# A graph and attention layer on one core: more buffers and later register reads in the routed stage, and both count matrices zeroed by SyncE

## What is computed

```python
xn = layernorm(x)
# two graph convolutions with symmetric normalisation and self loops
gnn = D^-1/2 (A+I) D^-1/2 relu(D^-1/2 (A+I) D^-1/2 xn W1 + b1) W2 + b2
# linear attention, 12 heads, 256 random features, then projection and layernorm
x = x + gnn + layernorm(xn + attention(xn) W_proj + b_proj) * gamma + beta
h = layernorm(x)
e = max(index of the two largest of h @ router_w)      # one of 8 experts per row
x = x + silu(h @ w1[e]) @ w2[e]
```

## Time and profile before

| | |
|---|---|
| median of 3 runs | 2644.51 us (2637.38 to 2648.0) |
| the profiled execution's own time | 2640.27 us |
| its span, first to last instruction | 2638.3 us |
| PE busy | 2413.7 us, 91% of the span |
| DVE, ACT, POOL busy | 1386.8, 802.2, 835.6 us |
| mean granted PE clock | 0.962 of full speed |
| DMA | 474.16 MB, mean 180 GB/s |

### The profile page before, as it was taken

One profiled execution on the slowest core, in us unless ns is written; L12 is line 12 of the kernel. 1 busy time (PEld: TensorE's weight loads), 2 busy tenths in 40 slices (PEclk: granted clock), 3 DMA queues, 4 the chain that ended last, 5 costly groups with the idle time before them and its releaser, 6 DMA issues.

```text
span 2638.3 us, 44428 instructions
## 1 busy us (share of the span) xinstructions
PE 2413.7 (91%) x16483; PEld 1628.1 (62%) x16483; DVE 1386.8 (53%) x2865; ACT 802.2 (30%) x1093; POOL 835.6 (32%) x587
## 2 busy tenths in 40 slices
PE   4889899999999999998899999999998899999376
PEld 2676768686866666666565566666664566666354
DVE  6575848583666767666313444444540444444343
ACT  3333324342364744646011222222220011111132
POOL 2133343435888888871000000000000000000265
PEclk9989989999999999999999999999998999999699
DMA  9976969654423233230432999999975844444186
GB/s 387 404 256 181 356 218 336 190 157 115 110 14 61 2 60 38 22 60 1 157 75 99 289 296 300 286 285 300 280 232 217 272 166 166 170 165 148 43 161 116
DMA packets 184192, 474.16 MB, mean 180 GB/s; under 512 B 74864, under 2 KB 81882, under 8 KB 174460
## 3 DMA queue, kind: packets, MB, share of 16 engines
q1 hardware_dynamic: 93596, 340.86, 36.6%
q0 software_dynamic: 79664, 101.99, 21.0%
q10 hardware_dynamic: 10800, 29.50, 2.9%
HBM read 266.99 MB, written 210.77 MB: 181 GB/s over the span
## 4 chain that ended last, share of the span: by engine, by line
PE 62%; DVE 13%; DMA 12%; ACT 6%; issue 4%; SPq 1%; POOL 0%; DVEq 0%; ACTq 0%; POOLq 0%
PE pair L1792 30%; PE pair L368 24%; DVE arena L1162 4%; DMA arena<-in_w_qkv 2%; PE pair L1617 2%; PE pair L1565 2%; DVE arena L1267 2%; DVE arena L1269 2%; DVE arena L1273 2%; DMA arena<-hl_dram,arena 2%; ACT arena L871 2%; DMA arena<-in_g_t 2%; PE pair L1628 1%; DMA arena<-in_ffn_in 1%; DMA arena<-ahl_dram 1%
## 5 line engine op out<-in xcount | busy, mean ns | idle before, releaser
L368 PE MATMUL pair<-arena 128*128 128x384 f16 (+2 forms) x5760 | 914.0, 320 | 27.6 <-SPq L357 7.2
L1792 PE MATMUL pair<-arena 128*128 128x384 f16 x4900 | 820.5, 328 | 25.9 <-DMA arena<-ahl_dram 11.8
L368 PEld LDWEIGHTS pair<-arena 128*128 128x128 f16 (+1 forms) x5760 | 570.0, 99 | 357.5 <-issue 34.0
L700 POOL DMA_INDIRECT cells<-arena x392 | 649.0, 1656 | 383.4 <-DMA cells<-arena 228.3
L1792 PEld LDWEIGHTS pair<-arena 128*128 128x128 f16 x4900 | 475.9, 98 | 336.3 <-issue 15.4
L1617 PE MATMUL pair<-arena 128*128 128x256 f32 x600 | 173.8, 425 | 18.9 <-ACT arena L810 18.9
L734 POOL DMA_INDIRECT slots<-arena x25 | 28.8, 1152 | 492.6 <-DVEq L1491 460.0
L1628 PEld LDWEIGHTS pair<-arena 128*128 128x128 f32 x1200 | 155.7, 197 | 20.1 <-ACT arena L835 15.1
L1628 PE MATMUL pair<-arena 128*128 128x66 f32 x1200 | 155.5, 278 | 11.1 <-ACT arena L835 11.0
L1162 DVE SCALAR_TENSOR_TENSOR arena<-arena 128x256 f16<-128x256 f32 x392 | 161.5, 479 | 4.7 <-DVE arena L1086 4.4
L722 POOL DMA_DIRECT2D arena<-cells x25 | 30.3, 1213 | 421.5 <-DMA arena<-cells 421.5
(11 more groups left out here) (195 smaller groups left out, 2270.4 us busy)
## 6 DMA issues: line engine op xcount, KB each, us to landing
cells<-arena POOLq DMA_DIRECT2D x25, 1600.0 KB, 11.1
cells<-arena SPq DMA_DIRECT2D x25, 1600.0 KB, 12.3
arena<-cells SPq DMA_DIRECT2D x25, 1600.0 KB, 9.6
arena<-cells POOLq DMA_DIRECT2D x25, 1600.0 KB, 13.2
ahl_dram<-arena SPq DMA_DIRECT2D x25, 1600.0 KB, 13.4
arena<-ahl_dram SPq DMA_DIRECT2D x25, 1600.0 KB, 7.6
arena<-in_x SPq DMA_DIRECT2D x70, 384.0 KB, 5.3
arena<-key_dram SPq DMA_DIRECT2D x28, 896.0 KB, 5.6
```

Of the source, the lines that this page charges most:

```text
L368: ins = nc.tensor.matmul(dst[half], left(k, a), right(k, b, half), start=start and n == 0, stop=stop and n == 2)
L700: nc.gpsimd.indirect_dma_start(cells[k], bass.IndirectOffsetOnAxis(ap=idx_all[:, m:m + 1], axis=0), val_all[:, m:m + 1], None, bounds_chec ...
L1792: ins = nc.tensor.matmul(pair[u][:, half, 0:HD], a[:, 0, s * P:(s + 1) * P], X[part][:, s, half * HD:(half + 1) * HD], start=(s == 0 and p ...
```

## The change

Three edits in one:

1. The routed stage has six gather buffers (NG) and four result buffers (NO). POOL issues gather(0..5) first, then for each j: add(j), gather(j+6). The buffers are zeroed as float32 (768 elements) and not as float16 (1536).
2. PE reads three expert registers before the first turn and each later one between an up and a down.
3. POOL zeroes nothing. SP issues all 50 strips in the 18 pairs of chunks 0 to 2, two or three after each weight load, matrix 0 first. Scatters start when matrix 0 is zero; BOTH is 4. Semaphores are shared in another way.

```diff
-BOTH = 8
+BOTH = 4
+CLEAR_CHUNKS = 3
+NG, NO = 6, 4
...
+            sp.wait_ge(consts, 2)
             for c in range(C):
...
-                    if c in (1, 2):
-                        for n in range(T * m // (2 * PAIRS) - T // 2, T * (m + 1) // (2 * PAIRS) - T // 2):
-                            clear_tile(sp, 1, n).then_inc(cleared_other, 16)
+                    if c < CLEAR_CHUNKS:
+                        for i in range(2 * T * m // (CLEAR_CHUNKS * PAIRS), 2 * T * (m + 1) // (CLEAR_CHUNKS * PAIRS)):
+                            clear_tile(sp, i // T, i % T).then_inc(cleared[i // T], 16)
...
-            for n in range(T):
-                if n >= 2:
-                    pool.wait_ge(cleared[n % 2], 16 * (n // 2))
-                clear_tile(pool, 0, n).then_inc(cleared[n % 2], 16)
-            all_cleared(pool)
+            all_cleared(pool, 0)
             for b in range(EDGE_UNITS):
                 if b == BOTH:
-                    pool.wait_ge(cleared_other, cleared_other_base + 16 * T)
+                    all_cleared(pool, 1)
...
-            for u in range(4):
-                made.link(nc.gpsimd.memset(g_in[u], 0.0))
+            for u in range(NG):
+                made.link(nc.gpsimd.memset(g_in32[u], 0.0))
...
-                if j >= 4:
-                    pool.wait_ge(g_tr, j - 3)
+                if j >= NG:
+                    pool.wait_ge(g_tr, j - NG + 1)
...
-            for j in range(4):
+            for j in range(NG):
                 gather_rows(j)
             for j in range(FT):
-                if j + 4 < FT:
-                    gather_rows(j + 4)
                 add_rows(j)
+                if j + NG < FT:
+                    gather_rows(j + NG)
...
             def result(j):
                 dve.wait_ge(f_y, j + 1)
-                if j >= 2:
-                    dve.wait_ge(added[j % 2], 16 * (j // 2))
-                nc.vector.tensor_copy(halves(fo[j % 2]), wide(2 + j % 2)).then_inc(f_out, 1)
+                if j >= NO:
+                    dve.wait_ge(added[j % NO], added_base[j % NO] + 16 * (j // NO))
+                nc.vector.tensor_copy(halves(fo[j % NO]), wide(2 + j % 2)).then_inc(f_out, 1)
...
-            expert = [pe.value_load(expert_i[0:1, j:j + 1], min_val=0, max_val=NX - 1) for j in range(FT)]
-            rows_turn(0, 0, 0)
-            rows_turn(1, 1, 0)
+            expert = {}
+
+            def read_expert(j):
+                expert[j] = pe.value_load(expert_i[0:1, j:j + 1], min_val=0, max_val=NX - 1)
+
+            for j in range(3):
+                read_expert(j)
+            rows_turn(0)
+            rows_turn(1)
...
+            for j in range(3, FT):
+                rows_turn(j)
                 up(j - 1, (j - 1) % 2)
+                if j + 1 < FT:
+                    read_expert(j + 1)
                 down(j - 2, j % 2)
```

More of the change, by code:

```diff
@@ L237, in build @@
         lnb = at(RT + 19104, 2, 16)
[L239 to L245, removed]
+        g_in = [at(RX + D * u, 2 * D, dt=F16) for u in range(NG)]
+        g_in32 = [at(RX + D * u, D) for u in range(NG)]
+        FR = RX + NG * D
+        fT = [[at(FR + HD * (2 * part + u), D, dt=F16) for u in range(2)] for part in range(2)]
+        hact = [at(FR + 1536 + P * u, P) for u in range(2)]
+        act_hi = [at(FR + 1792 + P // 2 * u, P, dt=F16) for u in range(2)]
+        act_lo = [at(FR + 1920 + P // 2 * u, P, dt=F16) for u in range(2)]
+        fo = [at(FR + 2048 + D * u, D) for u in range(NO)]
+        reach, reach_n = at(FR + 2048 + NO * D, FT, NX), at(FR + 2304 + NO * D, FT, NX)
         TAB = WST + 2304
@@ L324, in build @@
         consts, consts_in = sem("consts"), sem("consts_in")
[L325 to L329, removed]
+        edges_in, key_made = sem("edges_in_then_cleared0"), sem("key_made")
+        key_stored = sem("key_stored_then_cleared1")
+        cleared, cleared_base = [edges_in, key_stored], [64, 16]
+        strip_added = [sem(f"strip_added{u}_then_gathered") for u in range(2)]
+        scattered = [sem("scattered0_then_added"), sem("scattered1_then_slots")]
         rows_ld = [sem(f"rows_ld{q}") for q in range(4)]
@@ L373, in bank_halves, with all_cleared @@
             return [pair[i][:, h, 0:width] for h in range(2)]
-        def all_cleared(eng):
-            for u in range(2):
-                eng.wait_ge(cleared[u], 16 * ((T + 1 - u) // 2))
+        def all_cleared(eng, k):
+            eng.wait_ge(cleared[k], cleared_base[k] + 16 * T)
         zero_rows = zeros.rearrange("p (o f) -> p o f", o=1).to_broadcast([P, 5, 640])
@@ L755, in add_rows @@
                 nc.gpsimd.indirect_dma_start(
-                    out, bass.IndirectOffsetOnAxis(ap=ids[:, j:j + 1], axis=0), fo[j % 2], None,
-                    bounds_check=NP - 1, oob_is_err=False, compute_op=ALU.add).then_inc(added[j % 2], 16)
-            for j in range(4):
+                    out, bass.IndirectOffsetOnAxis(ap=ids[:, j:j + 1], axis=0), fo[j % NO], None,
+                    bounds_check=NP - 1, oob_is_err=False, compute_op=ALU.add).then_inc(added[j % NO], 16)
+            for j in range(NG):
                 gather_rows(j)
             for j in range(FT):
-                if j + 4 < FT:
-                    gather_rows(j + 4)
                 add_rows(j)
-            for u in range(2):
-                pool.wait_ge(added[u], 16 * (FT // 2))
+                if j + NG < FT:
+                    gather_rows(j + NG)
+            for u in range(NO):
+                pool.wait_ge(added[u], added_base[u] + 16 * (FT // NO))
         @block.scalar
@@ L785, in evict_hi @@
                 if n == (C - 1) * TC:
-                    all_cleared(act)
-                    act.wait_ge(cleared_other, cleared_other_base + 16 * T)
+                    for k in range(2):
+                        all_cleared(act, k)
                     act.wait_ge(far_st, 16)
@@ L1098, in evict_lo @@
                 if n == (C - 1) * TC:
-                    all_cleared(dve)
-                    dve.wait_ge(cleared_other, cleared_other_base + 16 * T)
+                    for k in range(2):
+                        all_cleared(dve, k)
                     dve.wait_ge(far_st, 16)
```

32 lines of the change are left out of this document (15 added, 17 removed).

## The result

The changed kernel takes 2609.32 us (median of 4 runs, 2607.57 to 2612.4), the one before 2646.26 us on the same chip (4 runs, 2637.38 to 2650.32). The ratio is 0.9866, with a 95% interval from 0.9838 to 0.9894: 1.3% faster, and clear of 1. The forecast was 2613 us in a range from 2593 to 2635. The profiled execution has a span of 2605.9 us (before 2638.3) at a mean granted clock of 0.969 (before 0.962).

The account below looks back on a forecast made before the run. PE is busy 91% of the span, so only stretches where it idles can give much. Start -7.5, pairs +1.2, first turn -10.3 and tiles -10.9 sum to -27.5 us: forecast 2613 us, range 2593 to 2635.

Parts of the forecast that it names:

- Start: Kernel start: without early strips, DVE's waits (2.15, 5.41 us) and PE's (7.07) go; first scan 7.5 us earlier, bounds 0 to 12.
- Pairs: Chunks 0 to 2: 19.1 us a pair, a strip 4.0, 6 us spilling into the value phase; net loss 1.2 us.
- Scatters: POOL's scatters, started when matrix 0 is zero, end between 1170 and 1235, covered by 80 to 140 us: cost 0.
- rival 4: Scatters end too late, layer 1 waits for counts: 65 us late, kernel 2678 us; chance 0.04.
- Rival 3: SP's ring overfull in chunks 0 to 2: 20 us a pair, no spill, kernel 2645 us; chance 0.10.
- First turn: Routed stage's start: with three reads ahead instead of 32, PE turns the first gather 10.3 us earlier.
- Per tile: Routed stage's 31 turns: 4.00 us a tile becomes 3.65, PE next on the bound; gain 10.9 us, bounds 0 to 21.7.
- A tile that never waits takes PE 3.06 us: Routed stage: PE's time for a tile without waits, read from the earlier trace, before the late read is added.
- 0.55 us is added: Routed stage: the read between up and down, 0.645 us less 0.1 of sequencer lead, brings PE's tile to 3.6 us.
- Rival 1: Routed stage: reads are hidden, POOL and DMA engines set 3.3 us a tile; 10.9 us better, 2602; chance 0.20.
- the way round: Routed stage: from gather to the add releasing the next, 4.1 us a tile, the bound before; 3.1 with six buffers.
- Tail: After the last turn: stays as it was, adds wait for POOL instead of buffers; gain 0.

Follow-up runs that it names:

- Experiment 12: Changed kernel with packed expert reads, two strips per pair in chunks 0 to 2 and 14 behind the x loads of value phases: 2585.48 us, ratio 0.9766 to the kernel before.
- experiment 4: Changed kernel with all 32 expert reads in front of the first turn: 2605.87 us, ratio 0.9843 to the kernel before.
- experiment 10: Changed kernel, but DVE packs eight experts into a word and PE reads four words ahead of the first turn: 2598.37 us, ratio 0.9814 to the kernel before.
- Experiment 7: Changed kernel without the adds of the routed stage, so the experts' results never reach the output; run once: 2590.22 us.
- experiment 5: Changed kernel with each late expert read between turn and up instead of between up and down: 2608.47 us, ratio 0.9842 to the kernel before.
- experiment 2: Changed kernel with four gather and two result buffers, POOL's old order and all reads in front: 2643.38 us, ratio 0.9977 to the kernel before.
- experiment 3: Changed kernel with four gather and two result buffers and POOL's old order, reads late: 2636.68 us, ratio 0.9937 to the kernel before.
- experiment 1: Kernel before with the changed routed stage (six and four buffers, POOL's new order, late reads), POOL still zeroing matrix 0: 2619.71 us, ratio 0.9886.

## Why the prediction was right, and where it was not

**Start.** The three waits went as said, 2.15 us to nothing, 5.41 and 7.07 to 0.77. The size was 10.2 for 7.5, inside the bound of 12. The waits gave 6.7 of it: PE's 144 matmuls start at 49.61 and not at 56.33. These matmuls then took 22.61 us at a granted clock of 1.00, before 24.71 at 0.91, behind the wait of 7.07 us: 2.1 us that the forecast had left out. The last 1.4 us lie between them and the first scan's end, where DVE before still made statistics of x tiles that had come late.

**Pairs.** The net loss was forecast at 1.2 us and measured at 1.5. The path to it was rougher than the figure. The forecast had pitches of 19.1 us and 6 us of spill into the value phase; measured were 18.0 us and value phases that hardly changed. Experiment 12 gives the price: 16.1 us with two strips, 18.0 with 2.78, so a third strip costs about (18.0-16.1)/0.78 = 2.4 us in its pair and not 4.0. That the rest fits into time the ring had left is argued, not shown. A spill and a price that were both too high made the right sum: that was luck.

**Scatters.** Hidden, with 94 us of cover (80 to 140 forecast), rival 4 was nowhere near. Rival 3 fell too: 18 us a pair, not 20.

**First turn.** Exact: 10.3, as all of it was read from rows (9.2 between experiment 4 and the changed kernel).

**Per tile.** 3.62 us measured over 31 turns against 3.65, and this is the step whose inside was wrong. "A tile that never waits takes PE 3.06 us" took a tile whose gather had only just come for one that never waits: that gather starts at 2602.71 and lands 5.0 us later, 0.05 us before the turn at 2607.80. Its up lasts 1.3 us. Where the gather has landed well before, an up lasts 1.00 and the tile 2.65. Experiments 4 and 10 show both kinds, and so did the trace before, on PE at the start of its routed stage:

```profile
2503.21 0.83 PE L1565 MATMUL pair<-arena 128*128 128x128 f16 x12
2503.88 1.17 PE L1923 MATMUL pair<-arena 128*128 128x128 f16 x18
...
2505.86 0.83 PE L1565 MATMUL pair<-arena 128*128 128x128 f16 x12
```

"0.55 us is added" priced the read from the earlier trace rows, where no add was in flight; beside adds the gap is 1.05. One term was 0.41 too high, the other 0.50 too low; that they cancelled was luck. Experiment 7 has both as they should have stood: quiet reads, and 3.2 us a tile.

The same error hid the main finding. Had the tile been put at 2.65, the sum would have shown that six buffers with reads in front come down to POOL's 3.15 to 3.3, and that late reads win 10.3 us (9.2 measured) only to lose 12.3: experiment 4 is as fast as the whole change. Rival 1 named the right floor (3.3) but the wrong way to it. The queue of 64 entries that the Trainium skill gives TensorE ("TensorE: Matmul & The Clock Gate", section "Architectural detail: the array is 16× 32×32, not 1× 128×128") did not hide a read at either place: 0.55 us was left behind twelve turning matmuls too (experiment 5).

The 4.00 us before were not the way round alone either, and the forecast has no term for the rest, though the earlier trace rows give the clock. In the 31 turns before, the granted clock was at half (1.2 GHz) for 13.6 us: until 2501.2, and again from 2511.4 to 2518.2, behind a wait of 4.04 us for a gather. In the changed kernel it was at half until 2483.0 only, 6.4 us. By my estimate that is up to 7.2/2 = 3.6 of the 11.9 us gained; how much of it waits for gathers would have absorbed isn't shown.

**Tail.** Costed at nothing, it gave 2.7 us. It goes with the buffers: 19.6 and 19.5 us in experiments 2 and 3 with four and two, 17.2 and 17.1 in 4 and 1 with six and four. Which of the two numbers does it wasn't tried, but the trace before points at the result buffers: after the last turn three copies on DVE wait 1.05, 1.00 and 1.34 us for an add to land, and in the changed kernel none does.

## What to carry to other kernels

A register read is priced where it will stand, not where it stood: by the adds in flight there and by what the array has queued ahead. If the values are small, pack them and read a word once. And in a DMA queue, bulk work belongs behind the loads that someone waits for: the same 14 strips lengthened the value phases by 22 us ahead of the x loads and not at all behind them, for 4 us in the pairs of chunk 1 (86.7 for 82.7) and 5 in those of chunk 3 (93.2 for 88.0).

## What the runs showed of the hardware

- A register read on PE's sequencer took 0.30 us when quiet and up to 1.2 us when made some 1.0 to 1.6 us after the end of POOL's instruction for an indirect add; in the changed kernel it then returned 2.1 to 2.5 us after that end. Later ones were short though adds were still under way, gathers did not lengthen it, nor did 215 GB/s of traffic in the one case shown. By which path they meet stays open. The Trainium skill, "DMA: Bandwidth & Descriptors", section "🔬 Latency and other measured facts", gives `tensor_load` a floor of about 600 ns. The trace has 293 ns for the instruction and 645 ns from one read to the next, with its address and limit instructions, so the trace agrees with that figure only for the pitch.
- A read cannot be passed: none of the matmuls behind it started before it returned, and the late reads left PE idle 0.39 us each even when short (experiment 7, by modelled ends; 0.55 by the starts).
- With the same 18 matmuls an up took 1.00 us in experiment 4 where its tile's gather had landed 0.4 us or more before the turn (up to 1.2 in experiment 10), and 1.2 to 1.6 in both where the turn before it had waited for the gather.
- The profile's releaser names can be wrong for an engine that was held by its own sequencer: "waits for DVE" and "waits for ACT" were register reads.
